# Layernorm statistics for blocks of four tiles, and half of the residual passes on VectorE

## The reference

```python
xn = _layernorm(x, axis=-1)
x = x + attn(xn) + ffn(xn)

def _layernorm(x, axis=-1, eps=1e-5):
    m = jnp.mean(x, axis=axis, keepdims=True)
    v = jnp.var(x, axis=axis, keepdims=True)
    return (x - m) / jnp.sqrt(v + eps)

# attn: c_q, c_kv = xn @ W_DQ, xn @ W_DKV (32 columns each), k_r = xn @ W_KR;
#       q, k, v from these for 8 heads, softmax over all 2048 keys, output projection
# ffn:  router scores, three Sinkhorn steps, top-2 gates; every expert computes
#       (relu(xn @ wg) * (xn @ wp)) @ wo; returns xn + gated sum of the experts
```

## Time and profile before

| what | us |
|---|---|
| two timed runs | 3979.28 and 4411.17, median 4195.23 |
| the profiled execution, whole | 3976.59 |
| its span on the slowest core (core 2), first to last instruction | 3975.1 |
| spans of the other cores | 3940.3 to 3966.4 |

### The profile page before, as it was taken

One profiled execution on the slowest core, in us unless ns is written; L12 is line 12 of the kernel. 1 busy time (PEld: TensorE's weight loads), 2 busy tenths in 40 slices (PEclk: granted clock), 3 DMA queues, 4 the chain that ended last, 5 costly groups with the idle time before them and its releaser, 6 DMA issues.

```text
span 3975.1 us, 43934 instructions; the slowest of 8 cores (3940.3 to 3975.1 us)
## 1 busy us (share of the span) xinstructions
PE 3597.7 (91%) x15210; PEld 1465.4 (37%) x15210; DVE 836.8 (21%) x1346; ACT 757.0 (19%) x1231; POOL 726.7 (18%) x1038
## 2 busy tenths in 40 slices
PE   2389999999999999898898999999999999999997
PEld 1133444444444444222222222344444444444443
DVE  3321211112121211122222222212121211211121
ACT  2420101010110101144444443011010101011010
POOL 1012222222222222100000000022222222222221
PEclk8599999999999999788888889999999999999999
DMA  4158788887878788600000000397878878787876
GB/s 68 39 51 114 70 109 79 108 98 90 109 77 117 69 110 85 98 1 1 1 1 1 0 1 1 69 106 80 114 73 111 79 107 96 91 111 77 119 66 131
DMA packets 618330, 290.70 MB, mean 73 GB/s; under 512 B 547324, under 2 KB 547357, under 8 KB 618118
## 3 DMA queue, kind: packets, MB, share of 16 engines
q0 software_dynamic: 610624, 271.03, 58.5%
q1 hardware_dynamic: 7494, 16.86, 1.2%
HBM read 550.39 MB, written 8.39 MB: 141 GB/s over the span
## 4 chain that ended last, share of the span: by engine, by line
PE 83%; DVE 6%; DMA 4%; ACT 3%; issue 3%; DVEq 0%; POOL 0%; SPq 0%; ACTq 0%; POOLq 0%
PE psum L609 21%; PE psum L541 21%; PE psum L549 21%; PE psum L772 4%; PE psum L768 4%; DMA s_areaC<-wexp 4%; DVE s_resid L631 3%; PE psum L758 3%; PE psum L762 3%; PE psum L803 2%; PE psum L660 1%; ACT s_areaB L778 1%; PE psum L342 1%; ACT s_areaB L703 1%; ACT s_areaB L710 1%
## 5 line engine op out<-in xcount | busy, mean ns | idle before, releaser
L609 PE MATMUL psum<-s_areaC,s_areaA 128*128 128x512 bf16 x4096 | 945.2, 392 | 105.3 <-DVE s_resid L631 73.2
L541 PE MATMUL psum<-s_xnT,s_wgbuf 128*128 128x512 bf16 x4096 | 968.9, 379 | 20.5 <-DVE s_resid L631 16.4
L549 PE MATMUL psum<-s_xnT,s_wpbuf 128*128 128x512 bf16 x4096 | 967.6, 379 | 0.0
L560 ACT ACTIVATE s_areaB<-psum 128x512 bf16<-128x512 f32 x512 | 305.7, 597 | 2464.2 <-PE psum L541 2463.9
L505 POOL DMA_DIRECT2D s_wgbuf<-wg x256 | 224.6, 877 | 2316.6 <-PE psum L541 2245.5
L609 PEld LDWEIGHTS psum<-s_areaC,s_areaA 128*128 128x128 bf16 x4096 | 407.1, 100 | 640.8 <-issue 194.8
L567 DVE TENSOR_TENSOR s_areaA<-s_areaB,psum 128x512 bf16<-128x512 bf16 x512 | 352.3, 688 | 1352.7 <-PE psum L549 1346.9
L541 PEld LDWEIGHTS psum<-s_xnT,s_wgbuf 128*128 128x128 bf16 x4096 | 399.4, 98 | 507.7 <-issue 30.1
L549 PEld LDWEIGHTS psum<-s_xnT,s_wpbuf 128*128 128x128 bf16 x4096 | 400.8, 98 | 483.3
L590 POOL DMA_DIRECT2D s_areaC<-wexp x512 | 271.9, 539 | 682.3 <-PE psum L609 680.5
L631 DVE SCALAR_TENSOR_TENSOR s_resid<-psum,s_w_tm,s_resid 128x512 f32<-128x512 f32 x256 | 192.1, 750 | 938.8 <-PE psum L609 915.4
(11 more groups left out here) (111 smaller groups left out, 726.5 us busy)
## 6 DMA issues: line engine op xcount, KB each, us to landing
s_areaC<-wexp POOLq DMA_DIRECT2D x512, 256.0 KB, 7.8
s_wgbuf<-wg POOLq DMA_DIRECT2D x256, 256.0 KB, 4.5
s_wpbuf<-wp POOLq DMA_DIRECT2D x256, 256.0 KB, 5.6
s_resid<-x SPq DMA_DIRECT2D x16, 512.0 KB, 3.3
y<-s_resid SPq DMA_DIRECT2D x2, 4096.0 KB, 13.0
s_areaC<-wo_attn POOLq DMA_DIRECT2D x1, 2048.0 KB, 18.0
s_wcat<-wdq POOLq DMA_DIRECT2D x1, 64.0 KB, 4.5
s_wcat<-wdkv POOLq DMA_DIRECT2D x1, 64.0 KB, 4.5
```

The source lines that it names most:

```text
L541: w.do("tensor", lambda t, c_=c, tb_=tb, tt2_=tt2, gs_=gs, b_=gb: t.matmul(bank(b_)[:, :], S["wgbuf"].ap()[:, gs_, c_, :], S["xnT"].ap()[: ...
L549: w.do("tensor", lambda t, c_=c, tb_=tb, tt2_=tt2, gs_=gs, b_=pbk: t.matmul(bank(b_)[:, :], S["wpbuf"].ap()[:, gs_, c_, :], S["xnT"].ap()[ ...
L560: w.do("scalar", lambda s, b_=gb, sl_=gp_count % 2: s.activation(out=Ebuf[:, sl_, :], in_=bank(b_)[:, :], func=AF.Relu), inc="sS")
L609: w.do("tensor", lambda t, f_=f, dh_=dh, tt_=tt, bk_=bk, ws_=ws, tb_=tb: t.matmul(bank(bk_)[:, :], hbuf[:, f_, tt_ * 128:(tt_ + 1) * 128], ...
```

## The change

Stage one now goes by blocks of four tiles. For a block the four loads, sums and squares come first; then the column operations and the root are done once for four tiles at a time, on [128, 4] columns of a larger `statc`, [128, 2, 4, 7]. The operation of line 297, which multiplied by the reciprocal and by -1 in one, is two operations now, since both factors are columns of a tensor. Then, tile by tile, come the normalising pass on ACT, the residual pass, the transposes and the copies. The residual pass is done by DVE for the first two tiles of a block, and by ACT, as before, for the other two. The projections that follow are as before. The wait of SP for the sum two tiles before is kept.

```diff
-        sb("statc", [128, 2, 8], F32)
+        sb("statc", [128, 2, 4, 7], F32)
...
-            for i in range(NT):
-                sl = i % 2
...
+            for B in range(NB):
+                bp = B % 2
+                if B >= 2:
+                    w.wait("vector", "sS", tok[("resid_v", (B - 2) * 4 + 3)])
+                for j in range(4):
+                    i = B * 4 + j
+                    sl = i % 2
+                    xs = "x0" if sl == 0 else "x1"
+                    if i >= 2:
+                        w.wait("sync", "vS", tok[("s1_v", i - 2)])
+                    w.do("sync", lambda q, i_=i: q.dma_start(
+                        out=S["resid"].ap()[:, i_, :], in_=dx[i_ * 128:(i_ + 1) * 128, :]),
+                        inc=xs, k=16)
...
+                    w.do("vector", lambda v, x_=xtile, j_=j: v.reduce_sum(
+                        stw[:, bp, j_, 0:1], x_, axis=AX.X), inc="vS")
+                    tok[("s1_v", i)] = w.tok("vS")
...
+                    w.do("scalar", lambda s, x_=xtile, j_=j: s.activation(
+                        out=sqout, in_=x_, func=AF.Square, accum_out=stw[:, bp, j_, 1:2]), inc="sS")
+                tok[("sq_s", B)] = w.tok("sS")
+                w.wait("vector", "sS", tok[("sq_s", B)])
+                w.do("vector", lambda v: v.tensor_scalar_mul(stw[:, bp, :, 2:3], stw[:, bp, :, 0:1], 1.0 / D), inc="vS")
...
+                w.do("scalar", lambda s: s.activation(
+                    out=stw[:, bp, :, 4:5], in_=stw[:, bp, :, 3:4], func=AF.Sqrt,
+                    bias=S["epsc"][:]), inc="sS")
...
+                w.do("vector", lambda v: v.reciprocal(stw[:, bp, :, 5:6], stw[:, bp, :, 4:5]), inc="vS")
+                w.do("vector", lambda v: v.tensor_tensor(stw[:, bp, :, 6:7], stw[:, bp, :, 2:3], stw[:, bp, :, 5:6], ALU.mult), inc="vS")
+                w.do("vector", lambda v: v.tensor_scalar_mul(stw[:, bp, :, 6:7], stw[:, bp, :, 6:7], -1.0), inc="vS")
+                w.do("vector", lambda v: v.tensor_scalar_add(stw[:, bp, :, 0:1], stw[:, bp, :, 5:6], 1.0), inc="vS")
...
+                for j in range(4):
...
+                    if i >= 2:
+                        w.wait("scalar", "tS", tok[("tr_t", i - 2)])
+                    w.do("scalar", lambda s, x_=xtile, j_=j, sl_=sl: s.activation(
+                        out=xnbf[:, sl_, :], in_=x_, func=AF.Identity,
+                        bias=stw[:, bp, j_, 6:7], scale=stw[:, bp, j_, 5:6]), inc="sS")
+                    tok[("xn_s", i)] = w.tok("sS")
+                    if j < 2:
+                        w.wait("vector", "sS", tok[("xn_s", i)])
+                        w.do("vector", lambda v, x_=xtile, j_=j, i_=i: v.tensor_scalar(
+                            S["resid"].ap()[:, i_, :], x_, stw[:, bp, j_, 0:1],
+                            stw[:, bp, j_, 6:7], ALU.mult, ALU.add), inc="vS")
...
+                    else:
+                        w.do("scalar", lambda s, x_=xtile, j_=j, i_=i: s.activation(
+                            out=S["resid"].ap()[:, i_, :], in_=x_, func=AF.Identity,
+                            bias=stw[:, bp, j_, 6:7], scale=stw[:, bp, j_, 0:1]), inc="sS")
```

More of the change, by code:

```diff
@@ new lines, in walk @@
+            NB = NT // 4
+            stw = S["statc"].ap()
+            for B in range(NB):
[11 more added lines that the diff above has]
+                        inc=xs, k=16)
+                    xtile = S["resid"].ap()[:, i, :]
+                    w.wait("vector", xs, 16 * (i // 2 + 1))
+                    w.do("vector", lambda v, x_=xtile, j_=j: v.reduce_sum(
+                        stw[:, bp, j_, 0:1], x_, axis=AX.X), inc="vS")
+                    tok[("s1_v", i)] = w.tok("vS")
+                    w.wait("scalar", xs, 16 * (i // 2 + 1))
+                    if B >= 2 and j == 0:
+                        w.wait("scalar", "vS", tok[("s1_v", i)])
+                    w.do("scalar", lambda s, x_=xtile, j_=j: s.activation(
[3 more added lines that the diff above has]
+                w.do("vector", lambda v: v.tensor_scalar_mul(stw[:, bp, :, 2:3], stw[:, bp, :, 0:1], 1.0 / D), inc="vS")
+                w.do("vector", lambda v: v.tensor_scalar_mul(stw[:, bp, :, 3:4], stw[:, bp, :, 1:2], 1.0 / D), inc="vS")
+                w.do("vector", lambda v: v.tensor_tensor(stw[:, bp, :, 4:5], stw[:, bp, :, 2:3], stw[:, bp, :, 2:3], ALU.mult), inc="vS")
+                w.do("vector", lambda v: v.tensor_tensor(stw[:, bp, :, 3:4], stw[:, bp, :, 3:4], stw[:, bp, :, 4:5], ALU.subtract), inc="vS")
+                tok[("var_v", B)] = w.tok("vS")
+                w.wait("scalar", "vS", tok[("var_v", B)])
+                w.do("scalar", lambda s: s.activation(
+                    out=stw[:, bp, :, 4:5], in_=stw[:, bp, :, 3:4], func=AF.Sqrt,
+                    bias=S["epsc"][:]), inc="sS")
+                tok[("sqrt_s", B)] = w.tok("sS")
+                w.wait("vector", "sS", tok[("sqrt_s", B)])
+                w.do("vector", lambda v: v.reciprocal(stw[:, bp, :, 5:6], stw[:, bp, :, 4:5]), inc="vS")
+                w.do("vector", lambda v: v.tensor_tensor(stw[:, bp, :, 6:7], stw[:, bp, :, 2:3], stw[:, bp, :, 5:6], ALU.mult), inc="vS")
+                w.do("vector", lambda v: v.tensor_scalar_mul(stw[:, bp, :, 6:7], stw[:, bp, :, 6:7], -1.0), inc="vS")
+                w.do("vector", lambda v: v.tensor_scalar_add(stw[:, bp, :, 0:1], stw[:, bp, :, 5:6], 1.0), inc="vS")
+                tok[("cols_v", B)] = w.tok("vS")
+                w.wait("scalar", "vS", tok[("cols_v", B)])
+                for j in range(4):
+                    i = B * 4 + j
+                    sl = i % 2
+                    xtile = S["resid"].ap()[:, i, :]
+                    if i >= 2:
[9 more added lines that the diff above has]
+                            stw[:, bp, j_, 6:7], ALU.mult, ALU.add), inc="vS")
+                        tok[("resid_v", i)] = ("vS", w.tok("vS"))
+                        tok[("resid_v", i)] = w.tok("vS")
+                        tok[("residv_is_v", i)] = True
+                    else:
+                        w.do("scalar", lambda s, x_=xtile, j_=j, i_=i: s.activation(
+                            out=S["resid"].ap()[:, i_, :], in_=x_, func=AF.Identity,
+                            bias=stw[:, bp, j_, 6:7], scale=stw[:, bp, j_, 0:1]), inc="sS")
+                        tok[("resid_v", i)] = w.tok("sS")
+                    w.wait("tensor", "sS", tok[("xn_s", i)])
+                    for c in range(8):
+                        b = (i * 8 + c) % 2
+                        w.wait("tensor", "vS", bank01[b])
+                        w.do("tensor", lambda t, c_=c, b_=b, sl_=sl: t.transpose(
+                            bankb(b_)[:, 0:128], xnbf[:, sl_, c_ * 128:(c_ + 1) * 128],
+                            S["eyeb"][:]), inc="tS")
+                        tk = w.tok("tS")
+                        w.wait("vector", "tS", tk)
+                        w.do("vector", lambda v, c_=c, b_=b, i_=i: v.tensor_copy(
+                            S["xnT"].ap()[:, c_, i_ * 128:(i_ + 1) * 128], bankb(b_)[:, 0:128]), inc="vS")
+                        bank01[b] = w.tok("vS")
+                        tok[("trev_v", i * 8 + c)] = w.tok("vS")
+                    tok[("tr_t", i)] = w.tok("tS")
+                i = B * 4 + 3
+                tn = B
```

## The result

The changed kernel takes 0.9919 of the time before, with a 95% interval of 0.9902 to 0.9936: 0.8% less, or 32 us of 3976.59 (25 to 39). The medians of all runs, 3945.91 us (11 runs, 3935.87 to 4472.54) against 4170.56 (10 runs, 3969.02 to 4514.52), don't show this, since 4 of the 11 and 5 of the 10 ran disturbed, with one die at a lower clock, and the ratio leaves those out. The profiled execution took 3944.32 us, with 3942.8 on its slowest core, which is core 5 now.

What follows compares the result with a forecast made beforehand. PE's matmuls fill 91% of the span; stage one before the FFN is a serial chain of hand-overs. Per block 7.13 + 4.07 + 15.39 = 26.59 us against 35.41, four blocks save 35.3: 3941.3 us, range 3910 to 3980.

Steps and rivals of the forecast that it cites:

- the prediction's four cases: Whole kernel: the forecast at 0.72, an earlier PE clock 0.14, the saving given back 0.08, late loads 0.06.
- 35.41 us a block before: Stage one, old order: traced time from a block's first sum on DVE to its last copy out of PSUM.
- 26.59 after: Stage one, new order: the same stretch of a block, summed from sums, column chain and copies; 8.82 us less.
- The sums, 7.13: Start of a block: four sums in a row on DVE, waiting for the third and fourth x loads; 7.13 us.
- The prediction's bound, 9.7: Upper limit for a block's four sums, if two loads of 3.6 us each came wholly one behind the other.
- The column chain, 4.07: From the last sum's end to the normalising pass's end, once per block: 3.80 us plus one operation of 0.27.
- The moved pass, 1.22: Residual pass of two tiles in four, moved from ACT into DVE's line; 1.22 us each, priced like the sum.
- The copies, 15.39 with two passes: End of a block: DVE's copies out of PSUM for four tiles, with two residual passes; 15.39 us.
- ACT delivers in time: Normalising passes of a block's third and fourth tiles stay hidden, done before DVE needs them, 2 us in hand.
- PE's clock rises earlier: Rival, chance 0.14: denser transposes lift PE's clock before the projections, saving another 2.6 us a block; 3930.9 us.
- The loads come late: Rival, chance 0.06: x loads in stage one land late, at 13.6 us making the kernel slower, 3982.6 us.
- The saving is given back: Rival, chance 0.08: something else, such as expert weights, sets the FFN's start; time stays at 3976.6 us.

## Where the prediction failed, and where it was right

What failed is the last step, from the gain to the chances. The prediction worked out a gain of 35.3 us, 0.9%, and then called it no change: "No case reaches 2% (80 us, which is about what a measurement of this kernel can tell from no change)" and "I leave 0.02 for each side", so 0.96 for no change. The runs showed a faster kernel: the ratio is 0.9919 with an interval of 0.9902 to 0.9936, and 0.9917 when the runs were repeated. The measurement tells far less than 2%, for its interval is 0.17% to either side. Two of the prediction's four cases, with 0.86 of its chances, lay at 0.991 and 0.989, far more than that below 1. The step also went against the prediction's own range, which rests on "one execution differs from another by some microseconds". A gain that was worked out term by term and is many times these microseconds should have been forecast as a faster kernel.

Before that step the account holds. The time, 3945.91 us, lies in the range, 0.1% over the forecast of 3941.3. The mechanism was right: stage one is one chain through DVE, batching shortens it, and what it gives leaves the span. That the time came so close is in part luck: two terms were mis-sized with opposite signs, the sums by 5.8 us too little in four blocks and the moved passes by 3.3 too much. Step by step:

- *35.41 us a block before* was 35.72 over all blocks; *26.59 after* was 27.50. So a block gave 8.22 where the prediction has 8.82, and four 32.9 where it has 35.3.
- *The sums, 7.13*: mis-sized. They took 8.57. Of the 1.44 us more, 0.34 lies before the third sum (4.93 after the first as a mean, 4.59 expected) and 1.10 before the fourth (2.42 after the third as a mean, 2.52 in the block shown, and not 1.32). "The landing is so steady" was read from loads 8.8 us apart, which never met. The prediction's bound, 9.7, held it. The run with loads four ahead shows that the whole excess over 5.29 is waiting for x.
- *The column chain, 4.07*: 4.12 in the block shown (74.98 to 79.10). Four columns cost 0.01 to 0.02 us more than one.
- *The moved pass, 1.22*: mis-sized, it takes 0.81. The nearest row was that of a reduction over the same tile, and it priced the wrong operation. The Trainium skill's table on "VectorE: DVE Perf Modes", section "The perf-mode tier table", sets such an operation at twice a reduction's rate, from which the estimate was 0.69. The trace's 0.81 is nearer to that than to the row's 1.22. The sign was right: all passes back on ACT are 5.7 us of stage better, and the pass alone makes the old kernel's blocks longer.
- *The copies, 15.39 with two passes*: 14.77 in the block shown. The two shorter passes take off 0.82; 0.20 comes back where a pair of copies comes apart near the end (92.31 and 92.84), and no run here says why.
- *ACT delivers in time*: as predicted, with 3.3 and 2.5 us in hand.
- *PE's clock rises earlier*: it did not. Over the tiles the granted clock is 0.50 (the 1.2 GHz level) as before, though PE's transposes come in pairs of 0.59 us with gaps of 0.22 for the most part of 14 us; it rises in the projections, as before, and their 24 matmuls take 7.51 us as a mean, 7.44 before. The same page of the Trainium skill, "TensorE: Matmul & The Clock Gate", has a closer rule than the one I cited, in its section "Part 4: PE-mode transpose": that transposes don't engage the full clock. The trace agrees, at 0.50. But plain matmuls with such gaps stayed at 0.50 in the attention stage too, and no run here tells apart whether the gaps or the kind of operation kept the clock down.
- *The loads come late*: the mechanism exists, but it costs 1.44 us a block over the 7.13, where 8.8 would have been needed to cancel the gain. Most of it comes from the neighbouring load on the same core, and not from the other cores as the rival had it.
- *The saving is given back*: not seen; see the ratios above.

## What to carry to other kernels

Batching small operations pays when they stand in a chain of hand-overs: here one root and eight column operations for four tiles, in place of one and seven for each, gave 38 us of stage (191.0 to 153.1). But check what the old order covered: four sums in a row need loads issued four ahead, not two, and moving work to the engine that the chain runs through costs time even if that engine is busy only a fifth of the span. The larger part of such a stage may lie in something the change left alone: here two copies for eight gave 29 us more (139.3 to 110.4).

## What the runs showed of the hardware

- Two loads of 512 KB issued 1.3 us apart landed 2.3 us apart as a mean (1.2 to 2.9; all cores, from the second block on). The one in front kept its time (3.47 us as a mean) and the one behind took 4.43 (3.8 to 5.3), where loads 8.8 us apart all landed within 3.8 (all cores, after 34 us). Issued in turn, the one behind took 3.50 again.
- DVE's scalar operation on 128x1024 f32 in SBUF takes 0.81 us, the sum over it 1.22, and ACT's pass 1.24.
- A DVE copy of 128x512 bf16 from PSUM takes 0.43 us, one of 128x128 0.225: four times the columns for 1.9 times the time, and each needs a hand-over besides.
- PE's transposes at a pitch of 0.81 us a pair for 14 us left the granted clock at 0.50.
